# Two transposes and two copies change places in a pipelined attention stack, and its mask is added by small products

## What is computed

```python
for i in range(DEPTH):                      # 6
    x = attn_layer(shift_tokens(x), Wqkv[i], q_scale[i], k_scale[i], Wo[i]) + x
    x = ffn_layer(shift_tokens(x), ln_g[i], ln_b[i], W1[i], b1[i], W2[i], b2[i]) + x

def attn_layer(x, Wqkv, qs, ksc, Wo):       # 16 heads of 64
    q, k, v = split(x @ Wqkv)
    q, k = l2norm(q) * qs, l2norm(k) * ksc  # then turned by the rotary tables
    out = local_attention(q, k, v)
    return out @ Wo

def local_attention(q, k, v):               # windows of 32 queries, 64 keys: own and previous window
    mask = (it < jb) | (it > jb + w) | (jb == -1)
    sim = einsum('bhwie,bhwje->bhwij', bq, bk2) * QK_SCALE
    sim = where(mask, -finfo.max, sim)
    attn = softmax(sim, -1)
    return einsum('bhwij,bhwje->bhwie', attn, bv2)

def ffn_layer(x, g, bln, W1, b1, W2, b2):   # 341 hidden channels
    a, gate = split((layernorm(x) * g + bln) @ W1 + b1)
    return a * gelu(gate) @ W2 + b2
```

## Time and profile before

| | |
|---|---|
| median of 3 runs | 4589.51 us (4580.05 to 4589.95) |
| the profiled execution | 4575.15 us, its span 4573.3 us |
| PE busy (matmul) | 4055.2 us, 89% of the span |
| POOL, DVE, ACT busy | 3001.9, 2776.7, 2723.2 us |
| mean granted TensorE clock | 0.954 of full speed |

### The profile page before, as it was taken

How to read it: one execution, slowest core, us unless ns; L and a number is a source line. 1 busy time by engine, 2 the same in 40 slices (tenths; PEclk the granted TensorE clock), 3 DMA queues, 4 the chain that set the end, 5 groups by cost and what they waited for, 6 DMA issues and landing times.

```text
span 4573.3 us, 164587 instructions
## 1 busy us (share of the span) xinstructions
PE 4055.2 (89%) x67239; PEld 2824.1 (62%) x67239; DVE 2776.7 (61%) x4602; ACT 2723.2 (60%) x5657; POOL 3001.9 (66%) x1858
## 2 busy tenths in 40 slices
PE   8989999999999999967999999999999997276975
PEld 5656666666666666635666666666666663153654
DVE  5556666666666666635666666666666663624541
ACT  5656666666666666634666666666666664134752
POOL 0068888888888888815888888888888882511001
PEclk9999999999999999989999999999999998587997
DMA  2023333333333333312333343333333331030004
GB/s 68 2 65 88 102 98 92 102 91 102 99 92 103 90 101 100 92 39 50 95 99 97 89 107 94 97 98 89 106 94 98 98 89 32 0 111 14 2 11 122
DMA packets 349821, 367.95 MB, mean 80 GB/s; under 512 B 58737, under 2 KB 285042, under 8 KB 348786
## 3 DMA queue, kind: packets, MB, share of 16 engines
q1 hardware_dynamic: 338834, 348.92, 29.2%
q0 software_dynamic: 2048, 4.20, 0.3%
q10 hardware_dynamic: 8160, 3.93, 0.3%
HBM read 247.12 MB, written 109.71 MB: 78 GB/s over the span
## 4 chain that ended last, share of the span: by engine, by line
PE 35%; ACT 8%; issue 3%; POOL 2%; DVE 2%; SPq 1%; DMA 1%; ACTq 0%; POOLq 0%; DVEq 0%
PE banks L325 6%; PE banks L386 3%; PE banks L309 3%; PE banks L330 3%; PE banks L430 2%; PE banks L369 2%; PE banks L292 2%; PE banks L845 1%; PE banks L424 1%; PE banks L863 1%; ACT arena L461 1%; PE banks L880 1%; PE banks L1311 1%; PE banks L1331 1%; ACT ln_rs L467 1%
## 5 line engine op out<-in xcount | busy, mean ns | idle before, releaser
L637 POOL TENSOR_TENSOR arena<-arena 128x512 f32<-128x512 f32 x768 | 960.4, 1272 | 522.6 <-DVE arena L566 401.6
L642 POOL TENSOR_TENSOR arena<-arena 128x1024 f32<-128x1024 f32 x384 | 905.9, 2359 | 30.1
L639 POOL TENSOR_TENSOR arena<-arena 128x1024 f32<-128x1024 f32 x384 | 907.8, 2364 | 0.0
L325 PE MATMUL banks<-w_qk,arena 128*128 128x512 f32 x1536 | 735.7, 602 | 15.5 <-DVE arena L666 10.6
L440 ACT COPY arena<-banks 128x512 f32<-128x512 f32 x384 | 224.3, 584 | 806.1 <-PE banks L386 806.1
L566 DVE SCALAR_TENSOR_TENSOR arena<-arena,banks 128x512 f32<-128x512 f32 x768 | 493.3, 684 | 308.1 <-ACT arena L474 306.6
L559 DVE TENSOR_REDUCE arena<-arena 128x8 f32<-128x512 f32 x768 | 494.2, 679 | 86.4 <-ACT arena L456 86.4
L533 DVE TENSOR_REDUCE arena<-banks 128x8 f32<-128x512 f32 x384 | 264.7, 689 | 399.9 <-PE banks L309 396.2
L456 ACT ACTIVATE arena<-banks 128x512 f32<-128x512 f32 x768 | 447.8, 596 | 82.8 <-PE banks L325 71.0
L325 PEld LDWEIGHTS banks<-w_qk,arena 128*128 128x128 f32 x1536 | 277.0, 193 | 271.6 <-issue 271.6
L386 PE MATMUL banks<-ident,arena 128*128 128x128 f32 x3072 | 424.7, 282 | 20.0 <-POOL arena L642 19.4
(11 more groups left out here) (220 smaller groups left out, 6715.1 us busy)
## 6 DMA issues: line engine op xcount, KB each, us to landing
v_rows<-arena SPq DMA_DIRECT2D x1536, 64.0 KB
arena<-v_rows SPq DMA_DIRECT2D x768, 128.0 KB
arena<-v_rows SPq DMA_DIRECT2D x768, 112.0 KB
arena<-in_moe_w SPq DMA_DIRECT2D x30, 515.5 KB, 3.8
w_qk<-in_stack_qk SPq DMA_DIRECT2D x48, 256.0 KB, 3.1
w_v<-in_stack_v SPq DMA_DIRECT2D x48, 128.0 KB, 3.4
w_o<-in_stack_o SPq DMA_DIRECT2D x12, 512.0 KB
w_w<-in_stack_w SPq DMA_DIRECT2D x12, 341.0 KB, 3.2
```

Of the source, the lines that this page charges most:

```text
L325: pe.matmul(bank(M, tile), f.sh[:, (s // G) % 2, o:o + 128], w.qk[:, g], start=True, stop=True).then_inc(S.qk, 1)
L637: nc.gpsimd.tensor_tensor(f.sined[:, :, :, half, :], x[:, :, :, 1 - half, :], sines[:, :, mine].unsqueeze(1).to_broadcast([D, GH, 4, DH // ...
L639: nc.gpsimd.tensor_tensor(rot, x.rearrange("p h t a d -> p h t (a d)"), cosines.unsqueeze(1).to_broadcast([D, GH, 4, DH]), ALU.mult).then_ ...
L642: nc.gpsimd.tensor_tensor(rot, rot, f.sined.rearrange("p h t a d -> p h t (a d)"), ALU.add).then_inc(S.rotated, 1)
```

## The change

It has two parts.

The mask: the two products of the whole array (128 rows, 128 columns, 256 wide, bfloat16) become eight of 64 rows by 32 columns, 256 wide: for each of the four groups of 32 PSUM partitions and each of the two banks, 32 columns of the identity pick the rows of a smaller mask table. The table holds window 0 and one other window in each half of the partitions; it is 128x256 rather than 128x512. A signal (`sem_inc`) that nobody waits for is put behind the waits and ahead of the products, as line 309 has one before.

The order: in steps other than 3 and 7 of a pair, TensorE's place 1 and the probabilities' transposes go ahead of the outputs' transposes; on ScalarE place 1 and the probabilities' copy go ahead of Ln and Exp, and the outputs' copy goes behind them. In steps 3 and 7 TensorE keeps its order; on ScalarE the outputs' copy goes ahead of the values' copy, the probabilities' copy ahead of Ln and Exp, and place 1 behind them.

```diff
@@ window_mask
-    m = np.zeros((D, 2, GH, KW), np.float32)
...
+    m = np.zeros((2, 2, WIN, 2, 2, KW), np.float32)
+    for w in range(2):
         for tile in range(2):
...
+            for q in range(WIN):
+                i, first = WIN * (w + 4 * tile) + q, WIN * (w + 4 * tile - 1)
+                j = first + np.arange(KW)
+                m[:, w, q, tile, :, (i < j) | (i > j + WIN) | (j < 0)] = NEG
+    return m.reshape(D, 2 * 2 * KW)
@@ pe_stack_step
         st.wait(S.normed, u - 1)
-        mask = M.wmask[:].rearrange("p (x b k) -> p x b k", b=2, k=KW)
-        for par in range(2):
-            pe.matmul(bank(M, 4 + par, T), M.identb[:], mask[:, :, par, :], start=True, stop=False,
-                      skip_group_check=True)
+        pe.sem_inc(M.s.pe_waited)
+        for c in range(4):
+            for par in range(2):
+
+                r, o = slice(64 * par, 64 * par + 64), 64 * par + 32 * min(c, 1)
+                pe.matmul(bank(M, 4 + par)[32 * c:32 * c + 32, 0:T], M.identb[r, o:o + 32], M.wmask[r, :],
+                          start=True, stop=False, skip_group_check=True)
...
+    if s % G == 3:
+
+        pe_stack_outs_turned(M, st)
+        pe_stack_probs_turned(M, st)
+    else:
+        pe_stack_hidden(M, st, 1)
+        pe_stack_probs_turned(M, st)
+        pe_stack_outs_turned(M, st)
...
+def pe_stack_outs_turned(M, st):
...
+        if not st.on(2):
+
+            st.wait(S.outs_taken, u)
@@ act_stack_step
+    if s % G == 3:
+        act_stack_outs(M, st)
+    if st.on(0):
+        u = s
         st.wait(S.v, u + 1)
...
+    if s % G != 3:
+        act_stack_hidden(M, st, 1)
+    if st.on(3):
+        u = s - 3
+        st.wait(S.probs_turned, u + 1)
+        st.wait(S.outs, u)
+        nc.scalar.copy(f.pt.rearrange("p t h k -> p (t h k)"), bank(M, 6)).then_inc(S.probs_taken, 1)
     if st.on(0):
         u = s
         st.wait(S.lengths, u + 1)
...
-    act_stack_hidden(M, st, 1)
-    if st.on(3):
-        u = s - 3
-        st.wait(S.probs_turned, u + 1)
-        st.wait(S.outs, u)
-        nc.scalar.copy(f.pt.rearrange("p t h k -> p (t h k)"), bank(M, 6)).then_inc(S.probs_taken, 1)
+    if s % G == 3:
+        act_stack_hidden(M, st, 1)
+    else:
+        act_stack_outs(M, st)
     act_stack_hidden(M, st, 2)
```

More of the change, by code:

```diff
@@ L372, in pe_stack_step, with pe_stack_probs_turned @@
     pe_stack_hidden(M, st, 2)
+def pe_stack_outs_turned(M, st):
+    pe, s, S, f = st.eng, st.s, M.st, stack_buffers(M)
+    if st.on(4):
+        u = s - 4
+        st.wait(S.normed, u + 1)
+        st.wait(S.heads_taken, u + 3 if st.on(2) else u + 2 if st.on(3) else u + 1)
+        if not st.on(2):
+            st.wait(S.outs_taken, u)
+        ov = f.o.rearrange("p (t h) d -> p t h d", t=2)
+        for hp in range(2):
+            for tile in range(2):
+                last = pe.transpose(bank(M, 3)[:, hp * T + tile * 128:hp * T + tile * 128 + 128],
+                                    ov[:, tile, 2 * hp:2 * hp + 2, :], M.ident[:])
+        last.then_inc(S.outs_turned, 1)
+def pe_stack_probs_turned(M, st):
+    pe, s, S, f = st.eng, st.s, M.st, stack_buffers(M)
+    if st.on(3):
+        u = s - 3
+        st.wait(S.probs, u + 1)
+        st.wait(S.probs_taken, u)
+        pv = f.p.rearrange("p (t h) k -> p t h k", t=2)
+        for tile in range(2):
+            for hp in range(2):
+                o = (2 * tile + hp) * 128
+                last = pe.transpose(bank(M, 6)[:, o:o + 128], pv[:, tile, 2 * hp:2 * hp + 2, :], M.ident[:])
+        last.then_inc(S.probs_turned, 1)
 def pe_stack_heads(M, st, qk):
@@ L461, in act_stack_step @@
         nc.scalar.copy(f.vt[:, u % 2].rearrange("p t a c -> p (t a c)"), bank(M, 2)).then_inc(S.v_taken, 1)
[L462 to L466, removed]
-        nc.scalar.copy(stack_hidden(M).ot[:, u % G].rearrange("p h t -> p (h t)"), bank(M, 3)).then_inc(S.outs_taken, 1)
+    if s % G != 3:
+        act_stack_hidden(M, st, 1)
+    if st.on(3):
+        u = s - 3
+        st.wait(S.probs_turned, u + 1)
+        st.wait(S.outs, u)
+        nc.scalar.copy(f.pt.rearrange("p t h k -> p (t h k)"), bank(M, 6)).then_inc(S.probs_taken, 1)
     if st.on(0):
@@ L474, in act_stack_step, with act_stack_outs @@
         nc.scalar.activation(f.rn[:, u % 2], f.lg, ACT.Exp, scale=-0.5).then_inc(S.inverse, 1)
-    act_stack_hidden(M, st, 1)
-    if st.on(3):
-        u = s - 3
-        st.wait(S.probs_turned, u + 1)
-        st.wait(S.outs, u)
-        nc.scalar.copy(f.pt.rearrange("p t h k -> p (t h k)"), bank(M, 6)).then_inc(S.probs_taken, 1)
-    act_stack_hidden(M, st, 2)
+    if s % G == 3:
+        act_stack_hidden(M, st, 1)
+    else:
+        act_stack_outs(M, st)
+    act_stack_hidden(M, st, 2)
+def act_stack_outs(M, st):
+    act, s, S, nc = st.eng, st.s, M.st, M.nc
+    if st.on(4):
+        u = s - 4
+        st.wait(S.outs_turned, u + 1)
+        if u % G == 0 and not (st.first and u == 0):
+            act.wait_ge(S.projected, st.f * 2 + u // G)
+        nc.scalar.copy(stack_hidden(M).ot[:, u % G].rearrange("p h t -> p (h t)"), bank(M, 3)).then_inc(S.outs_taken, 1)
 def act_stack_hidden(M, st, place):
```

31 lines of the change are left out of this document (3 added, 28 removed).

## The result

| | before | changed |
|---|---|---|
| median | 4588.40 us (4580.05 to 4589.95, 4 runs) | 4511.63 us (4505.26 to 4515.65, 4 runs) |
| profiled execution, its span | 4575.15, 4573.3 us | 4513.09, 4511.3 us |
| mean granted TensorE clock | 0.954 | 0.950 |

The ratio of the times is 0.9834 (95% interval 0.9819 to 0.9849): 77 us faster. The forecast was 4487 with a range of 4445 to 4550. The time is in the range, and 25 us above the forecast, which is more than the measurement can confuse.

A forecast was written before the change was run, and what follows sets the result against it. TensorE, busy 89%, was taken as the bound, held up 53.8 us by ScalarE's probabilities copy. Step terms gave -2.17 us a pair, -102 us over 47 pairs: 4473 us profiled, 4487 against the median, range 4445 to 4550.

The forecast's parts named there:

- Mask, -0.1 where nothing waits: Mask products ahead of the scores: eight small ones side by side take one streaming, 0.1 us less a step.
- The prediction's sign: In the changed profile, 0.2 us from the first mask product to the first score product.
- The serial mask: Rival: the eight mask products run one after the other, +0.65 us a step, +128 us, 4717; chance 0.03.
- four in a row: Rival: four mask products run serially on each half of the rows, +0.22 us a step, 4576 us; chance 0.05.
- the mask that gains nothing: Rival: the mask products take two streamings, so -1.6 us a pair, -76 us, 4513; chance 0.13.
- Steps 1, 2, 3, 5, 6, 7: Steps of a pair of 8: -0.1, -0.1, -0.2, -0.4, -0.65, -0.82 us from the mask and shorter waits.
- Step 2's lateness: VectorE's line 566 starts 2.5 us later in step 2; booked at nothing, as TensorE needs its result later.
- The first rival: Exp's lateness reaches TensorE through GpSimd and the head transposes: pair 1.2 us longer, +58 us, 4647; chance 0.07.
- Step 4: TensorE's last wait, line 402 behind ScalarE's 496 and VectorE's chain, stays; what is saved earlier is waited: 0.
- list of Exp's latenesses: Line 566 late by about 0.7, 0.6, 2.5, 0.9, 0, 0, 0.5, 0.9 us in steps 0 to 7, 6.1 in all.
- Step 0: Exp behind the copy makes line 566 0.58 to 0.75 us late, delaying the value product 430: a loss of +0.1.
- the sum: The eight steps' terms together: -2.17 us a pair, over 47 pairs -102 us.

The follow-up runs named there:

- e6: The kernel before with ScalarE's new order in steps 3 and 7 alone, TensorE as before; 4552.83 us, ratio 0.9928.
- e1: The kernel before with the eight small mask products alone, old order; 4573.28 us, ratio 0.9982.
- e8: The changed kernel with ScalarE running Ln and Exp ahead of the probabilities' copy in steps 0 and 4; 4475.97 us, ratio 0.9758.
- e9: The changed kernel with Ln and Exp ahead of the probabilities' copy in steps 0, 1, 2 and 4; 4478.79 us, ratio 0.9773.
- e5: e3 with 64 or 128 signals nobody waits for added on TensorE ahead of each call's first stack step; 4513.62 and 4528.77 us.
- e2: The changed kernel with the two full mask products and old table, so the order alone; 4522.44 us, ratio 0.987.
- e12: e8 with the two full mask products of before; 4495.36 us, ratio 0.9811.
- e4: The changed kernel with the mask in two products of 64 rows by 128 columns instead of eight; 4526.12 us, ratio 0.9879.
- e3: The changed kernel with the old order in steps 0 and 4 on TensorE and ScalarE; 4482.69 us, ratio 0.9779.

## Why the prediction held, and where it was off

**Mask, -0.1 where nothing waits.** Right, and by the working given: the eight start 3 ns apart, one streaming instead of two, and the 0.09 of the change of shape stays (the first score comes 0.12 after the mask instead of 0.31, but the mask comes 0.20 after the transposes instead of 0.11). The prediction's sign, 0.2 us from the first mask product to the first score, came out as 0.12 for that reason. The serial mask, four in a row and the mask that gains nothing are out, though the last has the measured time. The rule that the prediction cites from the Trainium skill (TensorE: Matmul & The Clock Gate, The mechanism), that a weight load overlaps running products only where its row group differs, does not hold in this trace: four of the eight share each row half, and all eight weight loads start within 0.03 us (923.058 to 923.081) while the first product runs (923.059 to 923.338).

**Steps 1, 2, 3, 5, 6, 7.** Forecast -0.1, -0.1, -0.2, -0.4, -0.65, -0.82; measured -0.01, -0.12, -0.24, -0.52, -0.60, -0.87. The reasons are those given. In step 5 GpSimd is what is late next (heads 0.05 behind it); e6 shows step 7's gain by itself, -0.76 without the mask. Only step 1 gained nothing, though e1 (7.04) and e8 (6.98) do gain there; why stays open.

**Step 2's lateness is covered.** Line 600 starts 2.5 us later in its step than 566 did, as worked out, and VectorE's wait for Exp grew over the span:

```profile
L600 DVE SCALAR_TENSOR_TENSOR arena<-arena,banks 128x512 f32<-128x512 f32 x768 | 493.6, 684 | 537.3 <-ACT arena L500 528.7
```

The page of before has 306.6 for it. The share of step 2 in these 222 us cost TensorE nothing (e9). The first rival had this lateness at its root and fell there.

**Step 4, forecast 0, measured +0.22: the step that failed.** The prediction said "That chain begins with the squares and lengths, which don't move." It does begin there, but Ln and Exp are links of it, and the change puts the copy ahead of them: Ln starts 4.81 after the projection (915.45 - 910.64) where it was 4.60 (928.32 - 923.72), and from scaling to 423 the chain takes 2.60 us in both (918.55 - 915.95, 931.41 - 928.81). The prediction had used exactly this for step 0 and for its list of Exp's latenesses, and put 0 for step 4 there too. The earlier trace rows show the end of the chain and not its beginning; the rows of ScalarE in step 4 weren't read in the new order. In substance it was the first rival, in a step it did not name and by another reader.

**Step 0, forecast +0.1, measured +0.24.** Line 600 is 0.74 late in its step (881.76 - 876.53 against 894.03 - 889.54), at the upper end of the 0.58 to 0.75 given, and 451 comes 0.14 late. The other 0.1 was not in the sum: 451 is now waited for, and then 0.96 us go from it to the next product (883.76 to 884.72) instead of 0.86 (896.63 to 897.49).

```profile
881.76 1.28 DVE L600 SCALAR_TENSOR_TENSOR arena<-arena,banks 128x512 f32<-128x512 f32 x2 [1.58 <-ACT arena L500]
882.96 0.74 DVE L632 SCALAR_TENSOR_TENSOR ln_sq<-banks,w_b,xc 128x512 f32<-128x512 f32 x1
883.76 0.30 PEld L451 LDWEIGHTS banks<-xc,w_w 128*128 128x128 f32 x2 [0.31 <-DVE ln_sq L632]
883.76 1.12 PE L451 MATMUL banks<-xc,w_w 128*128 128x512 f32 x2
884.72 1.88 PE L328 MATMUL banks<-w_qk,arena 128*128 128x512 f32 x4
```

Beyond the forecast the two steps lost 0.36 us of a pair, 17 us in 47 pairs; the other steps gave 4 of them back.

**The idle time with no releaser was in no term of the sum**: TensorE standing still 43 us before and 73 after, at a price of 12 to 30 us. The earlier trace rows show 17.2 and 5.1 us of it, and I passed over them. But those two are not what grew. The section on the kernel says that the steps are repeated over pairs and layers; in kernel.py the four pairs of a layer are written out, and layers 2 to 6 are a loop over them (`Fori` in `unit_steps`), so each call jumps back four times. Just behind each of the eight jumps TensorE stands still twice, in its first mask products and the small products after them. The jump into the third layer of the first call, before, and the two rows of the waits:

```profile
812.88 0.39 PE L283 MATMUL banks<-wmask,identb 128*128 128x256 bf16 x2 [0.72 <-issue]
813.20 0.44 PE L292 MATMUL banks<-arena 64*32 64x64 f32 x29
815.87 0.85 PE L292 MATMUL banks<-arena 64*32 64x64 f32 x35 [2.23 <-issue]
816.42 1.17 PE L309 MATMUL banks<-arena 64*32 64x64 f32 x64
```

```profile
PE banks L292 <- issue: 17.2, 8, 2.2
PE banks L283 <- issue: 5.1, 8, 1.0
```

That is 22 us in eight jumps before, 25 after, and 23 to 26 in every other kernel without added signals. After this jump the granted clock was 1.2 GHz for 3.4 us (815.8 to 819.2), which is why 309 takes 1.17 instead of 0.85. What grew is the rest, 21 to 48 us. Nearly all of it comes back in the same places: of the idle time in layers 2 to 6, 37 of 41 us before and 66 of 66 after lie in steps of the loop's body that stall in at least three of its five passes, and several of these steps differ between the two calls, whose program stands in two copies. So the stalls hang on the place in the program and hardly on what the step computes.

What speaks for program loading: TensorE's program comes in packets of 16 KB in the page's instruction queue. There are 552 of them in the kernels with the old mask and 571 in those with the eight products; 19 packets for 13 more instructions a step (6 products, 6 weight loads, the signal) make 62 bytes an instruction, an estimate. Of the stalls over 0.4 us in the stack, 36 before and 62 after, 28 and 54 end 1.2 to 1.6 us after such a packet has ended (ended, and not begun, as the expectation of e5 has it); of moments picked at random, 7 to 8% do. One of before, in the timeline, and the queue's row in the 3 us around it (945.5 to 948.5):

```profile
946.86 0.75 PE L309 MATMUL banks<-arena 64*32 64x64 f32 x52
948.31 0.33 PE L309 MATMUL banks<-arena 64*32 64x64 f32 x12 [0.71 <-issue]
```

```profile
q8 instruction: 1, 0.02, 1.8%
```

The second row starts after a stall, between the 52nd and the 53rd of 64 products that all have their data. Most come in the small products, where TensorE gets through most instructions in a microsecond. The new mask adds 6 products of that kind to each step, and a signal. With it 11 us came on (e1 over before), 19 (changed over e2) and 24 (e8 over e12); the order alone gave 2 to 11 (e12 and e2 over before). That the mask brings more idle time is shown by these three pairs. That it is the loading is argued from the places, the timing and e4; no run took the loading away. Why the order alone, with no instruction added, changes the sum stays open.

## What to carry to other kernels

When an operation is moved ahead of another on an in-order engine, follow in every step what the overtaken one starts, to the last reader, and read those rows in every step, also where the reader's own start of the chain seems fixed: one copy ahead of Ln cost 17 us more than forecast, beside the 77 won, and putting it back in the two steps whose reader waits won 29 to 36 us (e3, e8). Small products that run side by side save streaming time, but each is program to be fetched: in a kernel whose steps are written out, look for idle time without a releaser in the stretches of small products and behind the jumps of its loops, and book a price for more of them. And a saving ahead of a wait is no saving: the mask alone brought 0.2%, and twice that where nothing waits for the copy (e8 against e12).

## What the runs showed of the hardware

- Eight products of 64 rows by 32 columns, four on each half of the rows, start 3 ns apart and last 279 ns each (changed kernel, medians of 384 steps).
- A change of the products' shape on TensorE (full to 64x32, full to 64x128, 64x128 to 64x32) adds about 0.1 us, each time: 0.203, 0.205 and 0.213 us to the next start where 0.109 is usual (changed kernel and e4).
- Where the second value product (line 451) has been waited for, the projection starts 0.96 us after it, else 0.86 (changed kernel).
- A run of bare signals takes TensorE 0.18 to 0.21 us each (13.55 us for 64, 23.41 for 128).
- TensorE stood still with no releaser for 43 to 73 us over the stack, in pieces of mostly 0.4 to 2.5 us, most of which end 1.2 to 1.6 us after a packet of the instruction queue has ended.
- Behind each of the eight jumps of the layer loop it stood still for some 3 us (22 to 26 us in all), in every kernel without added signals.
